# A graph layer and a mixture of experts on one core: x1 of the last blocks stored by SP, clears and a turn moved ahead

## What is computed

```python
def reference(x, adj, L0_gnn_item_feat, ...):          # x: 10000 x 128, adj: 10000 x 10000
    def _L0_gnn_ref(user_feat, item_feat, adj, W_item, b_item, W_user, b_user):
        h = item_feat @ W_item.T + b_item
        b = user_feat @ W_user.T + b_user
        return jax.nn.relu(adj @ h + b)
    def _L0_ffn_ref(h, gate_w, gate_b, w1, b1, w2, b2):
        logits = x @ gate_w + gate_b                      # 8 experts
        idx, prb = the largest of softmax(logits)
        pos = the token's number within its expert; kept = pos < C     # C = 1563
        buf[idx, pos] = x                                 # kept tokens only
        hmid = relu(buf @ w1 + b1);  ybuf = hmid @ w2 + b2
        return nan_to_num(ybuf[idx, pos] * (prb * kept))
    x = x + _L0_gnn_ref(_layernorm(x), ...)               # called x1 below
    x = x + _L0_ffn_ref(_layernorm(x)[None], ...)[0]
    return x
```

## Time and profile before

| | us |
|---|---|
| median of 3 runs | 1337.58 (1336.89 to 1338.09) |
| the profiled execution | 1335.84 |
| its span, first to last instruction | 1334.0 |
| PE busy | 1302.6 (98%) |
| DVE busy | 1190.5 (89%) |
| ACT busy | 917.7 (69%) |
| POOL busy | 606.0 (45%) |

### The profile page before, as it was taken

How to read it: one execution, slowest core, us unless ns; L and a number is a source line. 1 busy time by engine, 2 the same in 40 slices (tenths; PEclk the granted TensorE clock), 3 DMA queues, 4 the chain that set the end, 5 groups by cost and what they waited for, 6 DMA issues and landing times. The chain is left out here.

```text
span 1334.0 us, 19239 instructions
## 1 busy us (share of the span) xinstructions
PE 1302.6 (98%) x5962; PEld 1070.9 (80%) x5962; DVE 1190.5 (89%) x1808; ACT 917.7 (69%) x840; POOL 606.0 (45%) x353
## 2 busy tenths in 40 slices
PE   8999999999999999999999999999999999899994
PEld 7788888888888888888888888888888888577772
DVE  6898999899999999999999999999999999677775
ACT  5666767667677677676676766776677665588772
POOL 5630072450633605326154161441624536867877
PEclk9999999999999999999999999999999999999998
DMA  9989999999999999999999999999999997343310
GB/s 361 355 340 383 405 382 386 400 369 370 394 386 400 369 377 400 379 401 371 383 404 379 400 375 395 404 394 398 386 389 384 383 375 275 92 117 99 83 45 5
DMA packets 101862, 446.67 MB, mean 335 GB/s; under 512 B 29029, under 2 KB 39539, under 8 KB 101815
## 3 DMA queue, kind: packets, MB, share of 16 engines
q1 hardware_dynamic: 74447, 423.00, 82.6%
q0 software_dynamic: 21408, 12.84, 3.8%
q10 hardware_dynamic: 5960, 10.24, 2.4%
HBM read 432.90 MB, written 23.88 MB: 342 GB/s over the span
## 5 line engine op out<-in xcount | busy, mean ns | idle before, releaser
L756 DVE TENSOR_TENSOR a_lo<-raw,a_hi 128x2000 fp32r<-128x2000 f32 (+1 forms) x400 | 868.4, 2197 | 48.4 <-ACT a_hi L573 45.5
L573 ACT CAST a_hi<-raw 128x2000 fp32r<-128x2000 f32 (+1 forms) x400 | 725.1, 1826 | 252.7 <-DMA raw<-adj_m 134.8
L1267 PE MATMUL bank<-a_hi,h_hi 128*128 128x500 f32 x1560 | 610.9, 392 | 4.9 <-POOL h_lo L1133 3.1
L1269 PE MATMUL bank<-a_hi,h_lo 128*128 128x500 f32 x1560 | 606.2, 389 | 0.0
L1278 PE MATMUL bank<-a_lo,h_hi 128*128 128x500 f32 x1560 | 419.7, 390 | 0.3 <-DVE a_lo L756 0.3
L1267 PEld LDWEIGHTS bank<-a_hi,h_hi 128*128 128x128 f32 x1560 | 293.5, 188 | 66.2 <-issue 7.2
L1269 PEld LDWEIGHTS bank<-a_hi,h_lo 128*128 128x128 f32 x1560 | 294.0, 188 | 57.9
L1278 PEld LDWEIGHTS bank<-a_lo,h_hi 128*128 128x128 f32 x1560 | 291.7, 188 | 58.6 <-DVE a_lo L756 0.9
L1148 POOL TENSOR_TENSOR late<-ve,neghalf 125x4 f32<-125x4 f32 x20 | 53.3, 2667 | 577.9 <-DVE ve L773 577.9
L1157 POOL DMA_INDIRECT records<-late,slot x80 | 179.1, 2239 | 22.6 <-issue 22.6
L1230 POOL DMA_INDIRECT out<-raw x101 | 135.5, 1342 | 39.3 <-issue 31.9
(11 more groups left out here) (149 smaller groups left out, 801.8 us busy)
## 6 DMA issues: line engine op xcount, KB each, us to landing
raw<-adj_m SPq DMA_DIRECT2D x379, 1000.0 KB, 11.0
raw<-adj_m SPq DMA_DIRECT2D x22, 500.0 KB, 5.9
xT<-x_t ACTq DMA_DIRECT2D x20, 250.0 KB, 9.8
spread<-user_rstd SPq DMA_DIRECT2D x20, 250.0 KB, 5.2
late<-items_t SPq DMA_DIRECT2D x19, 256.0 KB, 4.3
xb<-x ACTq DMA_DIRECT2D x20, 224.0 KB
raw<-records SPq DMA_DIRECT2D x14, 191.8 KB
raw<-records SPq DMA_DIRECT2D x9, 255.8 KB
```

The costliest lines, as they stand in the source:

```text
L573: last = nc.scalar.copy(a_hi[:, g % HI_RING, half:m], raw[:, g % RAW, half:m])
L756: last = v.tensor_tensor(a_lo[:, g % RAW, 0:m], raw[:, g % RAW, 0:m], a_hi[:, g % HI_RING, 0:m].bitcast(F32), ALU.subtract)
L1267: nc.tensor.matmul(acc[q][:, 0:BLOCK], h_hi[:, k * HID:(k + 1) * HID], a, start=(k == 0), stop=False)
L1269: last = nc.tensor.matmul(acc[q][:, 0:BLOCK], h_lo[:, k * HID:(k + 1) * HID], a, start=False, stop=False)
```

## The change

Four edits, all near the end of the stream and the start of the experts:

- POOL's `pass_on` of blocks 17 and 18 goes. SP stores x1 of both blocks whole (all 500 rows, kept or not) as it did for block 19: block 17 in the stream behind group 12 of block 19, block 18 behind `load_w2(0)`. The later output writes of kept tokens wait for all three stores. `take_x1` of block 19 waits for the store of block 17 in place of its pass_on.
- `set_zeros` and two of the eight clears stand ahead of `x1_scale(18)`; the other six and the edges behind it. `scatter(18)` is no longer split around `x1_scale(19)`.
- `load_w1(1)` stands right behind the read of the second expert's number, ahead of the records of units 4 and 5.
- Unit 3 is turned back sooner: `turn_y(3)` ahead of `turn_slots(5)` on the PE, `take_y(3)` ahead of `split_w1(1)` on ACT, and on DVE `gate_and_add(2)` ahead of `split_w1(1)` and `gate_and_add(3)` ahead of `slots_low(5)`.

The core of the diff:

```diff
+KEPT = 3
+AHEAD = 2
@@ SP
+                    if is_last(b) and g == 12:
+                        store_x1(b - 2)
...
+            def store_x1(n):
+                sp.wait_ge(x1_ready, n + 1)
+                sp.dma_start(out[n * BLOCK:(n + 1) * BLOCK, :].rearrange("(p j) d -> p j d", j=TILES),
+                             rec[:, n % 2, :, 0:HID]).then_inc(stored[BLOCKS - 1 - n], 16)
...
             load_w2(0)
+            store_x1(BLOCKS - 2)
...
                 if n == UNITS_E:
-                    store_last_x1()
+                    store_x1(BLOCKS - 1)
                     sp.wait_ge(order_ready, 2)
                     expert.append(sp.value_load(order_rest[0:1, 1:2], min_val=0, max_val=EXPERTS - 1))
+                    load_w1(1)
                     enough[n] = enough[n + 1] = landed(n + 1)
...
                 load_rec(n)
                 if n == UNITS_E + 1:
-                    load_w1(1)
                     load_w2(1)
@@ ACT, take_x1
-                    act.wait_ge(passed_on[q], pairs * (TILES * 16))
+                    if is_last(n):
+                        act.wait_ge(stored[2], 16)
+                    else:
+                        act.wait_ge(passed_on[q], pairs * (TILES * 16))
@@ ACT
             normalize_slots(4)
+            take_y(3)
             split_w1(1)
@@ DVE
             gate_and_add(1)
+            gate_and_add(2)
             split_w1(1)
             slots_low(4)
-            gate_and_add(2)
+            gate_and_add(3)
@@ POOL
+                if is_last(b):
+                    set_zeros()
+                    clear_slots(range(0, AHEAD))
                 if not fixed or b > 0:
                     x1_scale(b - 1, 1 - q)
...
                 if is_last(b):
-                    set_zeros()
-                    clear_slots()
+                    clear_slots(range(AHEAD, EXPERTS))
                     clear_edges()
-                    pool.wait_ge(slots_ready, b - 1)
-                    pass_on(q)
...
-            scatter(BLOCKS - 2, 0, range(0, 3))
+            scatter(BLOCKS - 2, 0)
             x1_scale(BLOCKS - 1, 1)
-            scatter(BLOCKS - 2, 0, range(3, TILES))
-            pass_on(0)
             scatter(BLOCKS - 1, 1)
-            pool.wait_ge(stored, 16)
+            for last in range(KEPT):
+                pool.wait_ge(stored[last], 16)
@@ PE
             turn_y(2)
             turn_slots(4)
+            turn_y(3)
```

More of the change, by code:

```diff
@@ L72 @@
 BEYOND = 1.0e6
+PASSED = [len(range(q, BLOCKS - KEPT, 2)) for q in range(2)]
 ALL_OF_17 = (BLOCKS // 2 - 1) * TILES * 16
@@ L313, in build @@
         dve_rest_chain = sem("dve_rest_chain")
-        stored = sem("stored")
+        stored = [sem(f"stored{i}") for i in range(KEPT)]
         sent = [sem(f"sent{i}") for i in range(YRING)]
@@ L529, in _ @@
                     load_w2(r)
-            sp.wait_ge(passed_on[0], BLOCKS // 2 * TILES * 16)
-            sp.wait_ge(passed_on[1], (BLOCKS // 2 - 1) * TILES * 16)
-            sp.wait_ge(stored, 16)
+            for q in range(2):
+                sp.wait_ge(passed_on[q], PASSED[q] * TILES * 16)
+            for last in range(KEPT):
+                sp.wait_ge(stored[last], 16)
             for u in range(YRING):
@@ L717, in step @@
                     take_mid(at - LAG_MID)
[L718 removed]
+                if has(at, LAG_Y, 4):
                     take_y(at - LAG_Y)
```

20 lines of the change are left out of this document (7 added, 13 removed).

## The result

The changed kernel takes 1342.03 us (median of 5 runs, 1341.73 to 1344.53) against 1337.58 for the kernel before: a ratio of 1.004, with a 95% interval of 1.0029 to 1.0051, or 4.45 us more. The forecast was 1337.9 with a range up to 1340.6, so the time lies outside it, on the slower side. The profiled execution took 1342.03 us (span 1340.2), which is 6.19 more than that of before (1335.84).

What follows compares the result with a forecast made beforehand. The PE, busy 98% of the span, was taken as the bound. Later turn_slots(5) +0.66 and turn_y(3) in the gap -0.33 gave +0.33; added to the 1337.58 median as 0.3: 1337.9 us, range 1335.7 to 1340.6.

Steps and rivals of the forecast that it cites:

- clears and store at nothing: Last block's stream of adj: earlier clears and block 17's store were taken as 0 us on the path.
- the rival of the late stream: Last adj loads delayed 2 to 5 us, deciding from some 5 us; would cost about 3 us, 1341; chance 12%.
- Clears land 4 us sooner: POOL's clears ahead of the scatters: landing 4 us sooner, so scatter 17 starts near 1127 and not 1130.84.
- by nothing: Lower bound on how much sooner POOL's clears land, as the DMA engines are full; the upper bound was 5 us.
- The count and the settle stall: PE's count 0.37 us sooner and DVE's long first settle instruction gone, 0.36: together 0.73 us sooner up to turn_y(2).
- The gap at turn_slots(5): PE idles until DVE's slots_low(4), behind gate_and_add(2) and w1's split; turn_slots(5) starts at 1165.05, not 1164.39.
- +0.66: Later start of turn_slots(5) on the PE in us, with the 0.73 gained earlier already in it.
- The slow clock stays in my sum: PE's low clock behind the gap at turn_slots(5) stays as before, since the gap is no shorter.
- The rival in which the clock holds: PE clock not lowered around turn_slots(5), as turn_y(3) works inside the gap: 1.5 us saved, 1336.4; chance 15%.
- The base: Start of the sum: profiled execution of before, 1335.84 us, with the median taken to lie 1.74 above it.

Runs made afterwards that it cites:

- b2: Kernel before with only the second expert's w1 load moved ahead of the two loads of records: 1335.99 us, ratio 0.9994 to before.
- e2: Changed kernel with the fourth unit's order undone on PE, ACT and DVE: 1338.47 us, ratio 1.0001 to before.
- e1: Changed kernel run once more, unchanged, as the mark on its chip: 1341.24 us, ratio 1.0023 to before.
- d1: Changed kernel with block 17's store behind the stream, the fourth unit's old order, and four clears ahead of block 18's power: 1338.02 us, ratio 1.0007 to before.
- a5: Changed kernel with clears back behind the power, block 17's store behind the stream and the fourth unit's old order: 1338.09 us, ratio 1.0009 to before.
- e4: Changed kernel with block 17's store behind the stream and the fourth unit's old order: 1339.17 us, ratio 1.0001 to before.
- a1: Changed kernel with memsets and all eight clears back behind block 18's power, store still in the stream: 1346.5 us, ratio 1.0034 to before.
- a3: Changed kernel with all clears back behind block 18's power and block 17's store behind the stream: 1345.4 us, ratio 1.0017 to before.
- a2: Changed kernel with block 17's store moved behind the stream, early clears kept: 1342.69 us, ratio 1.0001 to before.
- c2: Changed kernel, unchanged, run again beside the kernel before on another chip: 1345.22 us, ratio 1.0011 to before.
- f1: Kernel before with w1 ahead of the records and two clears ahead of block 18's power: 1341.98 us, ratio 0.9987 to before.
- c1: Kernel before, unchanged, run again for its trace on another chip: 1343.18 us, ratio 0.9993 to before.
- fourth comparison: Follow-up on one chip of the changed kernel, two kernels with parts of it undone, and the kernel before with w1 ahead and the new order; before took 1338.18 us.
- f2: Kernel before with w1 alone moved ahead of the records, run a second time: 1342.74 us, ratio 0.9986 to before.
- e3: Kernel before with w1 ahead of the records and the fourth unit's new order, nothing else: 1338.47 us, ratio 1.0000 to before.
- a4: Changed kernel with the fourth unit's order undone, clears and store as changed: 1341.15 us, ratio 0.9988 to before.
- c3: Changed kernel with block 17's store behind the stream and the fourth unit's old order: 1339.81 us, ratio 0.9974 to before.

## Why the prediction was wrong, point by point

| PE, in the traces | turn_slots(5) behind turn_y(2) | turn_slots(5) to end of span |
|---|---|---|
| before, old order, w1 behind | 3.97 | 169.61 |
| b2, old order, w1 ahead | 2.74 | 169.24 |
| e2, old order, w1 ahead | 3.04 | 169.93 |
| e1, new order | 5.50 | 169.59 |
| after, new order | 5.51 | 170.57 |

**The step that failed: clears and store at nothing.** The prediction put the earlier clears and the store of block 17 at 0 on the path, because ACT's last cast waited for DVE and not for a load. In the changed kernel that cast came 6.8 us later. ACT's lead hid 4.4 of them; the last load held `turn_slots(0)` back by 2.45 us, and 3.4 us at the lower clock followed, so that `turn_x1(19)` started 4.45 us later (1141.08 against 1136.63). This was the rival of the late stream. Its mechanism came as described, its condition too ("a delay of some 5 us"): all three traces with clears ahead of an on-time stream show it, so its 12% were too little, and its 3 us were less than these 4.45. That the clears have a part in it is shown by d1 against a5, with four clears. How it divides between the two clears and the store of the change stays open: e2 and e4 do not differ in time, and the store may cost 1 to 2 us where the stream is late (a1 against a3, a2 against c2, the latter on two chips), hardly more than the noise.

**"Clears land 4 us sooner"** was wrong as well: 1.1 us. The first clear was issued 7.3 us sooner (1089.32 against 1096.6), but the edges, behind the last of them, only 2.3 (1110.53 against 1112.87). The clears shared the DMA engines with the loads, and q1 alone had filled these before. Against before, the prediction's bound "by nothing" was the nearer end; against a5, with the clears behind the power and no other change on POOL, they landed 5.0 us sooner.

**The count and the settle stall.** Taken by themselves they came true. POOL had issued its scatters and waited for DVE ahead of the power (1.70), the count ran without a wait, and the row that answers to the earlier trace rows has no long one:

```profile
L982 DVE TENSOR_SCALAR over<-pos x20: 161/164/170, 162.2 to 1150.9; 125x4 f32<-125x4 f32 x20
```

Up to `turn_y(2)` from the start of `turn_x1(19)` (1141.08 after, 1136.63 before) the changed kernel needs 23.04 us and the one before 23.79: 0.75 gained, 0.73 forecast. That POOL waited for DVE there is in part because the PE was late.

**The gap at turn_slots(5)** was right in size: 1165.05 - 1159.69 = 5.36 us behind `turn_y(2)` forecast, 5.51 measured, released by DVE's `slots_low(4)`, with `turn_y(3)` ahead of it. DVE started at 1164.65, once `turn_y(2)` was done, for which it had waited 1.76 us. What the prediction did not draw out is how much shorter the gap is with w1 ahead alone: 2.74 us in b2, 2.74 to 3.40 in the nine such traces, 3.04 in the mean, against 5.24 to 5.51 and 5.47 in the mean in the seven with the new order. It counted +0.66 against before, where w1 was late; against its own other edit the order costs 2.4 - 0.33 = 2.1 us and buys nothing. e1 against e2 measured 2.8.

**The clock.** "The slow clock stays in my sum" took the same 3.4 us at 1.2 GHz behind a longer gap. In the profiled execution it was 6.8, and this is the 0.96 of the last piece. Of seven traces with the new order two have 6.8 us there (after and a3) and five 3.4; from `turn_slots(5)` to the end the two took 170.57 and 170.63 us, the five 169.20 to 169.62. So it is a cost of some executions, about 1.2 us. The rival in which the clock holds came in none of these seven, and it was mis-sized: in f1, with the old order, the clock did hold, behind a wait of 1.82 us,

```profile
1168.00:1172.00 4.00, 2.18 (x14) 1.73 (x13) 3.64 (x7) 2.36 (x6) 3.35 (x3) 1.00 0.63 142
1172.00:1176.00 4.00, 3.24 (x17) 2.37 (x16) 1.69 (x6) 3.26 (x7) 3.39 (x3) 1.00 0.60 181
```

and `turn_slots(5)` to the end took 169.54 us. With b2 (169.24) and e2 (169.93), where it held too, that is 169.57 in the mean; six traces with the same gap and a fall took 169.69 to 170.02, 169.94 in the mean. The next unit waits for ACT or DVE where the clock holds (`turn_slots(6)` 0.65 us in b2 and f1, 0.83 in e2): by these few traces, which overlap (e2's 169.93 lies among the six), some 0.4 us are gained, not 1.5.

**The base.** The profiled execution of before, 1335.84, is below all five timed runs of it on that chip (1336.5 to 1338.19), with a stream that had caught up. The 1.74 up to the median was carried over as a constant; c1 suggests that part of it is executions in which the stream was late for the kernel before too. That was not measured on the chip of the forecast, and how the 4.45 us divide there stays open by that much. On the chip of the fourth comparison, with before at 1338.18, they divide as: order 2.8 us; w1 about -1 (from b2 and f2, on other chips); clears, missing pass_on and whole stores together about +1.3, to make 0.3 without the order and 3.1 with it. This takes the parts to add up, which e3 with its smaller cost of the order puts in doubt. In the forecast's terms, by an estimate from these numbers, the sum without the order would have been -0.73 for the count and the settle and -0.9 for w1 (3.97 - 3.04), some -1.7; e2 took +0.3, 2.0 more, and that is the term put at nothing, here too. The order was some 2.1 in those terms (the gap's 2.4, less 0.33), and took 2.8.

## What to carry to other kernels

Read a stream's slack over its whole length and in more than one execution: that nobody waits for it at the end does not say how much more it can carry, and work moved ahead of its last transfers is paid by them. When two edits aim at the same wait, work out each one alone as well: here one load moved gave about a microsecond, and the new order behind it took two or more away. Where an in-order engine gets a long step in front of a short one that the bound engine waits for, the short one goes first even if the long one is ready.

## What the runs showed of the hardware that was not expected

- The kernel before took 1337.1 to 1343.5 us in the median in the six comparisons, and 1336.02 to 1349.11 within the last of them. On those with the higher medians the traces have ACT waiting for `adj` into the last blocks; the loads of 1000 KB take 10.0 to 13.3 us from issue to landing between 860 and 1080 us, against 6.6 to 7.5 where the stream has caught up. The DMA engines' busy share is full in both (1.00 to 1.02 in c1 and in before).
- Behind equal waits of 1.82 us the granted clock fell in six traces (a4, a5, c3, d1, e4, f2) and held in three (b2, e2, f1). Where it fell it was low for some 3.4 us. It was low for some 6.8 behind the waits of 4.65 to 4.97 us at `turn_slots(0)`, and as long behind the count's waits of 2.88 us in a5 and 1.18 in b2, so the length of the wait alone does not tell how long it stays low.
